# An attention layer's running sums moved behind the key and query scalings, and GpSimd's inverse roots moved one tile sooner

## The reference, cut to what matters

```
q = _l2norm(q) * q_scale
k = _l2norm(k) * k_scale
sim = jnp.einsum('bhid,bhjd->bhij', q, k) * ATTN_SCALE
...
sim = sim + dist[None, None] * slopes[None, :, None, None]
causal_mask = cols[None, :] > rows[:, None] + NUM_NULL_KV
neg = -jnp.finfo(sim.dtype).max
sim = jnp.where(causal_mask[None, None], neg, sim)
attn = jax.nn.softmax(sim, axis=-1)
out = jnp.einsum('bhij,bhjd->bhid', attn, v)
out = out.transpose(0, 2, 1, 3).reshape(b, n, HEADS * DIM_HEAD)
return out @ w_out
```

## Time and profile before

| What | Value |
|---|---|
| Median of 3 runs | 1959.13 us (1958.53 to 1962.52) |
| The profiled execution | 1963.62 us, span 1961.9 us |
| Busy, share of the span | PE 84%, DVE 56%, ACT 39%, POOL 29% |
| Attention's 16 turns | about 72 us to 1262 us of the span |
| Mean granted TensorE clock | 0.906 of 2.4 GHz |

### The profile page before, as it was taken

One profiled execution on the slowest core, in us unless ns is written; L12 is line 12 of the kernel. 1 busy time (PEld: TensorE's weight loads), 2 busy tenths in 40 slices (PEclk: granted clock), 3 DMA queues, 4 the chain that ended last, 5 costly groups with the idle time before them and its releaser, 6 DMA issues. The chain is left out here.

```text
span 1961.9 us, 28499 instructions
## 1 busy us (share of the span) xinstructions
PE 1645.5 (84%) x8973; PEld 771.4 (39%) x8974; DVE 1095.6 (56%) x2591; ACT 757.7 (39%) x1250; POOL 564.3 (29%) x557
## 2 busy tenths in 40 slices
PE   5899999999999999999999999745964777776777
PEld 2344444344443444444444444344642332232332
DVE  4454555556556646546546656562225666666664
ACT  2445445445445444444454454302421222322231
POOL 4243253352352442442542533152012011110000
PEclk8799999999999999999999999857985887887788
DMA  3602022022022021021120100041110000000000
GB/s 95 183 1 63 1 63 73 1 62 63 1 62 73 1 63 54 10 62 34 30 62 4 59 4 1 1 160 46 47 41 11 0 11 11 11 11 6 0 6 11
DMA packets 106705, 73.63 MB, mean 38 GB/s; under 512 B 5249, under 2 KB 100761, under 8 KB 106318
## 3 DMA queue, kind: packets, MB, share of 16 engines
q1 hardware_dynamic: 104526, 67.76, 11.3%
q0 software_dynamic: 2048, 4.20, 0.7%
HBM read 24.23 MB, written 47.71 MB: 37 GB/s over the span
## 5 line engine op out<-in xcount | busy, mean ns | idle before, releaser
L718 ACT ACTIVATE P<-S,keyb 128x386 f32<-128x386 f32 (+7 forms) x512 | 296.8, 630 | 417.9 <-PE S L514 405.1
L510 PE MATMUL S<-QT,KT 64*128 64x512 f32 (+5 forms) x1792 | 377.3, 477 | 12.6 <-DVE KT L856 10.9
L1036 POOL TENSOR_TENSOR rn<-nm,half 128x12 f32<-128x12 f32 x128 | 324.1, 2542 | 9.8 <-DVE nm L793 9.8
L891 DVE TENSOR_TENSOR Psum<-Psum,P 128x1796 f32<-128x1796 f32 (+7 forms) x256 | 286.7, 1120 | 35.9 <-PE O L534 18.3
L1052 POOL TENSOR_SCALAR_AFFINE_SELECT P<-P 128x256 f32<-128x256 f32 (+1 forms) x256 | 119.7, 468 | 626.9 <-ACT P L718 626.9
L534 PE MATMUL O<-P,V 128*64 128x512 f32 (+5 forms) x1536 | 259.8, 441 | 14.1 <-POOL P L1052 12.1
L510 PEld LDWEIGHTS S<-QT,KT 64*128 64x128 f32 (+1 forms) x1792 | 157.8, 180 | 203.9 <-issue 195.3
L167 POOL TENSOR_TENSOR norm_rstd<-norm_vareps,half 128x4 f32<-128x4 f32 x32 | 32.8, 1024 | 460.4 <-DVE norm_vareps L152 460.3
L405 PE MATMUL W<-xT,wts 128*128 128x512 f32 x256 | 144.5, 661 | 9.7 <-DVE QT L852 7.2
L514 PE MATMUL S<-GQ,GK 64*128 64x512 bf16 (+5 forms) x896 | 149.9, 303 | 0.0
L913 DVE TENSOR_TENSOR part<-W,rden 128x512 f32<-128x512 f32 x128 | 82.3, 684 | 91.0 <-PE W L582 91.0
(11 more groups left out here) (219 smaller groups left out, 2233.3 us busy)
## 6 DMA issues: line engine op xcount, KB each, us to landing
xg<-zero SPq DMA_DIRECT2D x16, 1216.0 KB, 7.2
yg<-zero SPq DMA_DIRECT2D x16, 1216.0 KB, 10.7
wts<-in_w_qkv SPq DMA_DIRECT2D x16, 384.0 KB, 3.8
gu<-in_gu SPq DMA_DIRECT2D x1, 2816.0 KB, 9.8
xb<-xg SPq DMA_DIRECT2D x40, 64.0 KB, 1.8
yg<-yb SPq DMA_DIRECT2D x40, 64.0 KB, 1.6
X<-in_x SPq DMA_DIRECT2D x4, 512.0 KB, 4.5
wo<-in_w_out SPq DMA_DIRECT2D x16, 128.0 KB, 2.3
```

Of the source, the lines that this page charges most:

```text
L510: nc.tensor.matmul(S[hh][0:m, at + c:at + c + w], KT[d, r, p, jt * P:jt * P + m], QT[d, r, p, Q0[jt] + c:Q0[jt] + c + w], start=True, stop ...
L718: nc.scalar.activation(probs(p, jt)[0:m, hh, 0:n], S[hh][0:m, at:at + n], ACT.Exp, bias=keyb[0:m, r, (2 * p + hh) * NKT + jt:(2 * p + hh) ...
L891: nc.vector.tensor_tensor(x, x, probs(p, jt)[0:m, :, 0:NQ[jt]], ALU.add).then_inc(add_ok, 1)
L1036: nc.gpsimd.tensor_tensor(rn[:, c, u], nm[:, c, u], powers, ALU.pow).then_inc(rn_ok, 1)
```

## The change

DVE's sums of tiles 11, 12 and 15 (tiles counted from 0, so they stand in steps 12, 13 and 16) move. Before, the sum of tile 11 stood at the end of step 12 and that of tile 12 at the end of step 13. Now both stand at the end of step 13, and the sum of tile 15 stands behind the scaling of S11 in step 16. GpSimd's roots move: for the first half from behind the cuts of tiles 5, 6, 7 and 8 to behind those of 4, 5, 6 and 7; for the second half from behind tiles 10 (three roots) and 11 to behind tiles 8, 9 (two roots) and 10. No instruction is added or taken away, and PE's, ACT's and SP's orders are the same.

```diff
-                        late = s in (12, 13)
-                        if s and (s - 1) % NKT and not late:
+                        late = {12: (), 13: (11, 12), 16: (15,)}
+                        if s and (s - 1) % NKT and s not in late:
                             add(t, (s - 1) // NKT, (s - 1) % NKT)
...
                         if ahead:
                             prepare(t + 1, 1 - r, f"{s}b")
-                        if late:
-                            add(t, (s - 1) // NKT, (s - 1) % NKT)
+                        for k in late.get(s, ()):
+                            add(t, k // NKT, k % NKT)
...
                 def prepare(n, s):
 
-                    for c, u, at in ((0, 0, 5), (0, 1, 6), (0, 2, 7), (0, 3, 8), (1, 0, 10), (1, 1, 10), (1, 2, 10), (1, 3, 11)):
+                    for c, u, at in ((0, 0, 4), (0, 1, 5), (0, 2, 6), (0, 3, 7), (1, 0, 8), (1, 1, 9), (1, 2, 9), (1, 3, 10)):
                         if s == at:
                             root(n, c, u)
```

## The result

The changed kernel takes 1945.8 us (median of 6 runs, 1939.4 to 1950.3) against 1959.9 before (6 runs, 1956.9 to 1963.8): a ratio of 0.9924, 95% interval 0.9903 to 0.9945. It is faster, by 14 us or 0.8% where I forecast 32 us, and the time lies just above the range that I gave. The profiled execution took 1947.5 us with a span of 1945.7, against 1963.6 and 1961.9.

What follows compares the result with a forecast made beforehand. PE was taken to bound the attention's turns, so only its waits could be won: 15 turns at 1.8 us give 27, plus 5 from the clock, 32 us off the 1959.1 median, forecasting 1927 us, range 1912 to 1945.

Steps and rivals of the forecast that it cites:

- What bounds the kernel: PE bounds the attention's turns; only its waits at three places, together 3.5 us a turn, can be won.
- The roots: Moving GpSimd's roots earlier gets the cuts of tiles 9, 10 and 11 in time, removing PE's 0.61 us wait.
- The sums: Moved DVE sums remove S02's 1.90 wait, add 1.2 before S10; with the roots, 1.8 us a turn taken.
- The clock: Of 10.8 us lost to half-clock stretches in 14 turns, half, 5 us, comes back once the long wait goes.
- My own sign of being wrong: The prediction would be wrong if, among other signs, the clock fell in most turns' last stretch.
- slower by the clock: Rival, chance 0.06: waits moved to a turn's last 4 us drop the clock every turn, 2.9 us each; 1965 us.
- The other rivals: Besides one part alone: gain given back whole, tile 14's cut held until the third sum's end; chance 0.07, about 1959 us.
- one of the parts alone works: Rival, chance 0.12: only the roots' or only the sums' move pays; 1942 to 1950 us.

Runs made afterwards that it cites:

- filled: The changed kernel plus four throwaway matmuls that PE runs in its wait before S10: 1924.3 us, ratio to before 0.9830.
- before_filled: The kernel before the change plus twenty small throwaway matmuls in PE's wait before S02: 1956.8 us, ratio to before 0.9969.
- roots_only: The kernel before the change with only GpSimd's roots moved, DVE's sums left in place: 1972.5 us, ratio to before 1.0073.
- filled_again: The changed kernel with four throwaway matmuls ahead of S10, timed a second time: 1923.1 us, ratio to before 0.9813.
- filled_elsewhere: The changed kernel plus the same four matmuls ahead of projection P10 in step 5, where PE has no wait: 1961.1 us, ratio to before 0.9998.
- sums_only: The kernel before the change with only DVE's sums moved, GpSimd's roots left in place: 1962.8 us, ratio to before 1.0013.
- sums_filled: The kernel before the change with only DVE's sums moved, plus four throwaway matmuls ahead of S10: 1933.5 us, ratio to before 0.9863.
- rt_first_filled: Changed kernel, tile 13's sum behind RT, tiles 14 and 15's behind S11's scaling, three throwaway matmuls before tile 15's values: 1919.1 us, ratio to before 0.9796.
- rt_first: The changed kernel with tile 13's sum behind RT and tiles 14 and 15's behind S11's scaling: 1935.3 us, ratio to before 0.9887.

## Why the prediction was wrong

**What bounds the kernel: right.** What the turns won came out of PE's waits at the three places; PE's busy time in a turn without a fall stayed (70.98 and 71.07 us).

**The roots: right.** The wait of 0.61 is gone, the cuts of tiles 9, 10 and 11 come in time, and GpSimd's being held for `nm` costs PE nothing. With the clock kept up the roots are worth 0.7 us a turn.

**The sums: right in mechanism, a little small in size.** S02's wait is gone, `RT` became the new bound with 0.92 (forecast 1.2), and 0.52 is left before the first scores (forecast about 0.5). Both parts together are worth 2.0 us a turn where I took 1.8. The filled kernels show it free of the clock: 1051.4 less 1024.4 is 27.0 us over 14 turns, and by their ratios to before the two kernels are 27 to 31 us apart, where 15 × 2.0 is 30.

**The clock: wrong, and wrong in sign.** The step that failed is "With the long wait gone and two shorter ones elsewhere, I count half of the 10.8 back: 5 us". Instead the 14 turns lose 21 us (1044.2 less 14 × 73.1 is 20.8), 10 more than before, and the part from the last turn's start on took 758.1 us instead of 754.9, 3.2 more. The sum in the profiled executions: 14 turns give 28 (14 × 2.0) by the waits and lose 10 by the clock, which is 18; what lies ahead of them gives 1.4 (144.80 against 143.40); the tail takes 3.2. That is 16.2, the difference of the spans. My own sign of being wrong, a fall in most turns' last stretch, came true.

Of the 3.2 us, 0.8 belong to the change, and my sum had no term for them. The last turn prepares no next one, so it has nothing to win; but its sums have moved too, and PE waits longer there for GpSimd's cuts (3.3 us in place of 2.6). Windows of the last turn, before and after:

```profile
1207.00:1260.90 53.90, 49.61 (x361) 22.22 (x362) 31.17 (x39) 24.75 (x40) 9.11 (x18) 1.00 0.00 1
1187.60:1242.40 54.80, 49.69 (x366) 22.30 (x364) 31.47 (x40) 24.70 (x40) 10.27 (x18) 1.00 0.00 1
```

The last turn takes 54.7 to 54.8 us in all the kernels with the sums moved, and 53.9 in before, before_filled and roots_only. The other 2.4 us lie in the layers behind it, where the same kernel, filled and filled_again, took 697.7 and 700.6 us: that is the spread between executions.

I had this as the rival *slower by the clock*, at the place where it happened, with a chance of 0.06, and had priced it at 2.9 us a turn. The price came to 21 / 14 = 1.5 us a turn, so against before the clock took back 10 us of the 28, about a third, and not all of it. The 2.9 came from a fall of 6.8 us; 11 of the 12 falls here last 3.4. What led me astray was to judge a stretch by its longest single wait. In the last 5 us of a turn a wait of 0.92 is enough for what a wait of 1.90 did before. filled shows it: four matmuls in that wait, and no fall is left, though the wait of 0.52 stays. filled_elsewhere shows that the count of matmuls doesn't do it. That the stretch is sensitive because its matmuls are small is my reading; no run replaced them by larger ones.

**The other rivals: rightly set aside.** The cut of tile 14 was not kept out until the third sum's end (806.79 above), and neither part fails. But with one part alone the clock makes the time that of before or worse; *one of the parts alone works* gave 1942 to 1950 us, where sums_only took 1962.8 and roots_only 1972.5.

**Open.** Before the change, the same wait of 1.90 was followed by a fall in five turns and by none in the others; with roots alone, where the turn is 0.6 shorter, in all fifteen. So where the waits stand in time matters too, and I haven't found by what rule. One regularity is in the record of the granted clock: in the changed kernel nearly all falls come 75.1 us behind the one before (885.4, 960.5, 1035.6, 1110.7), or about twice that where a turn has none. A turn of before without a fall takes 75.1 us as well, and eight of them follow each other without one (377.6 to 978.7). So before may owe its few falls to the length of its turn, which would be luck, and a shorter turn may have lost it; no run separates this from the waits. In the four profiled executions with the wait in the last stretch filled whole (filled twice, sums_filled, rt_first_filled; 72.9 to 73.8 us a turn) no turn had a fall.

## What to carry to other kernels

Where PE is the bound, price a reordering twice: by the waits that it takes away, and by how full PE is in the stretch to which the remaining waits move. Here waits of 0.92 and 0.52 us in a turn's last stretch cost another 1.3 to 1.9 us where the clock fell, and in the kernel before no fall stood behind the wait of 0.61 at tile 11. Try the edit with throwaway matmuls in the new wait before judging it: here the sums alone, worthless by their time (1962.8), came to 1933.5 us, and turns without a fall priced the two parts at 1.3 and 0.7 us each.

## What the runs showed of the hardware that I had not expected

- Taking 0.61 us of waiting out of each turn made the kernel 0.7% slower (interval 0.5 to 1.0), by falls of the clock in 15 turns instead of 6.
- The granted clock fell to 0.50 behind a stretch in which PE was busy in 2.24 of 3.10 us, and in filled_elsewhere behind a single wait of 0.92 us.
- Matmuls on constants whose result nothing reads, 0.8 us a turn in a wait, brought about 20 us (0.9924 to 0.9830 and 0.9813 of before). The same matmuls where there was no wait cost 15.
- A DVE sum that runs holds up a GpSimd cut until its end: 1.75 us for one of 0.40 in the changed kernel, and 0.69 us of waiting on PE in rt_first. The Trainium skill, SBUF — State Buffer, section "Who interferes with whom", states that exclusion, and the traces agree where the sum is the first: the cut was let in at the sum's end each time.
- The traces don't agree with that exclusion where a GpSimd root is the first. In the trace of before, a sum that started 0.54 us into a root took no longer than the 0.70 of one beside no root or cut, and the root took its usual 2.27:

```profile
788.05 2.27 POOL L1036 TENSOR_TENSOR rn<-nm,half 128x12 f32<-128x12 f32 x1
788.59 0.69 DVE L891 TENSOR_TENSOR Psum<-Psum,P 128x516 f32<-128x516 f32 x1
```
